# Attention's constants and its first batch prepared inside the expert phase of a two-layer kernel

## The reference, cut to what matters

```python
# layer 0: experts (8 routed, 2 shared), then a ternary projection, added to x
gp = _leaky(jnp.einsum('th,ehm->etm', x, w_gate))
up = jnp.einsum('th,ehm->etm', x, w_up)
y_all = jnp.einsum('etm,emh->eth', gp * up, w_down)
...
x = x + _L0_ffn_ref(_L0_cond_ref(...), packed_weight, weight_scale, bias)

# layer 1: attention, 16 heads of 64, one shared key and value head, one "null" key and value
xn = layernorm(x, g_in)
q = (xn @ Wq).reshape(b, n, H, DH).transpose(0, 2, 1, 3) * scale
kv = xn @ Wkv
k = jnp.concatenate([nk, k], axis=1)      # nk, nv: the null key and value
sim = jnp.einsum('bhid,bjd->bhij', q, k) + bias     # causal and padding masks follow
attn = jax.nn.softmax(sim, axis=-1)
out = jnp.einsum('bhij,bjd->bhid', attn, v)
return layernorm(out.reshape(b, n, INNER) @ Wo, g_out)
...
x = x + _L1_ffn_ref(...)                  # a quantised feed-forward layer
```

## Time and profile before

| | us |
|---|---|
| median of 3 runs (lowest, highest) | 1431.74 (1431.39, 1432.29) |
| the profiled execution | 1432.46 |
| its span in the trace | 1430.5 |

### The profile page before, as it was taken

How to read it: one execution, slowest core, us unless ns; L and a number is a source line. 1 busy time by engine, 2 the same in 40 slices (tenths; PEclk the granted TensorE clock), 3 DMA queues, 4 the chain that set the end, 5 groups by cost and what they waited for, 6 DMA issues and landing times. The chain is left out here.

```text
span 1430.5 us, 29675 instructions
## 1 busy us (share of the span) xinstructions
PE 1251.0 (87%) x8705; PEld 996.3 (70%) x8710; DVE 1029.2 (72%) x2788; ACT 771.5 (54%) x1948; POOL 553.6 (39%) x834
## 2 busy tenths in 40 slices
PE   3999999999945799999999999999999999944866
PEld 2778888888832578777887887778788788831223
DVE  5566666666553877887887778877878878763986
ACT  3223323333312576766776767667667677625853
POOL 1333332333331775444453454444444444500014
PEclk9999999999975899999999999999999999976986
DMA  6233221221025100000000010010010000202115
GB/s 230 70 127 104 83 76 48 103 88 61 28 81 194 53 5 2 1 28 5 2 30 4 2 31 2 1 33 2 1 31 1 17 2 2 76 16 63 59 59 176
DMA packets 51039, 71.52 MB, mean 50 GB/s; under 512 B 4497, under 2 KB 43665, under 8 KB 48850
## 3 DMA queue, kind: packets, MB, share of 16 engines
q1 hardware_dynamic: 50338, 69.60, 14.7%
q10 hardware_dynamic: 560, 0.20, 0.1%
HBM read 57.07 MB, written 12.72 MB: 49 GB/s over the span
## 5 line engine op out<-in xcount | busy, mean ns | idle before, releaser
L864 POOL TENSOR_SCALAR scores<-scores,att_rinv 128x128 f32<-128x128 f32 (+3 forms) x512 | 264.2, 532 | 195.7 <-DVE att_rinv L1076 195.7
L920 ACT ACTIVATE scores<-scores,att_top 128x128 f32<-128x128 f32 (+3 forms) x512 | 281.5, 553 | 77.4 <-DVE att_top L1058 77.1
L1058 DVE CUSTOM_DVE_ANT_0 scores<-ps_y,w_bias_b,null_s 128x128 f32<-128x128 f32 x448 | 229.7, 548 | 83.3 <-PE ps_y L1208 76.8
L271 POOL TENSOR_TENSOR act_w<-act_g,wide_w 128x512 f32<-128x512 f32 x64 | 105.7, 1652 | 261.2 <-DVE act_g L393 255.6
L1207 PE MATMUL ps_y<-k_hh,q_hl 128*128 128x256 f32 (+2 forms) x512 | 190.1, 380 | 14.7 <-DVE att_top L1058 7.3
L928 ACT ACTIVATE keep<-ps_up 128x128 f32<-128x128 f32 (+3 forms) x256 | 112.1, 438 | 167.8 <-PE ps_up L1219 163.9
L1219 PE MATMUL ps_up<-ident,scores 128*128 128x128 f32 x1280 | 190.8, 274 | 9.8 <-DVE keep L1086 9.1
L215 ACT ACTIVATE hid_hi<-hid 128x512 fp32r<-128x512 f32 x80 | 50.6, 632 | 233.9 <-DVE hid L411 229.6
L1219 PEld LDWEIGHTS ps_up<-ident,scores 128*128 128x128 f32 x1280 | 151.3, 141 | 30.9 <-issue 13.7
L1230 PE MATMUL ps_a<-keep,w_val 128*64 128x128 f32 x2560 | 170.7, 280 | 0.7 <-DVE keep L1086 0.7
L871 POOL TENSOR_SCALAR w_q_hm<-q_hl 64x512 fp32r<-64x512 f32 x128 | 76.7, 611 | 228.5 <-ACT q_hl L943 228.5
(11 more groups left out here) (237 smaller groups left out, 2581.6 us busy)
## 6 DMA issues: line engine op xcount, KB each, us to landing
wide_w<-token_w_dram SPq DMA_DIRECT2D x16, 1024.0 KB, 4.7
x_raw<-in_x_t_dram SPq DMA_DIRECT2D x8, 512.0 KB, 3.8
x_nat<-in_x_nat_dram SPq DMA_DIRECT2D x8, 512.0 KB, 4.8
x_dram<-x_nat SPq DMA_DIRECT2D x8, 512.0 KB, 2.9
w_x1t<-x_dram SPq DMA_DIRECT2D x8, 512.0 KB, 4.3
c_dram<-out_raw SPq DMA_DIRECT2D x8, 512.0 KB, 3.2
c2t<-c_dram SPq DMA_DIRECT2D x8, 512.0 KB, 3.7
x_tile<-x_dram SPq DMA_DIRECT2D x8, 512.0 KB, 4.5
```

Source lines behind the costliest of these rows:

```text
L271: nc.gpsimd.tensor_tensor(act_w[:, k % 2], act_g[:, k % 2], wide_w[:, k], ALU.mult).then_inc(sem.act_w_ready, 1)
L864: nc.gpsimd.tensor_scalar(s, s, rinv[:, pp, q, hh:hh + 1], 0.0, ALU.mult, ALU.add).then_inc(sem.p_normed, 1)
L920: nc.scalar.activation(s, s, ACT.Exp, scale=-1.0, bias=top[:, pp, q, hh:hh + 1], accum_out=lsum[:, pp, q, hh:hh + 1]).then_inc(sem.exp_don ...
L1058: dve.tensor_tensor_reduce(scores_of(pp, hh, q), psS[:, hh, 0:n], bias_of(w, h)[:, CAUSAL[q]:CAUSAL[q] + n], 1.0, null_s[:, par, q, h:h + ...
```

## The change

There is no `setup_attention` any more. Its work and attention's serial piece are put into `moe_phase`:

- **The experts' first batch** (`not behind`) gets the constants. DVE signals `raw_free` when the raw expert weights have been split. SP issues `load_projections` behind batch 0's `load_nat`, before `spread_weights(1)`. POOL fills after expert 2 and makes `null_prod` in halves after experts 4 and 6; DVE: `null_picks` behind expert 2, `projections_lo` behind 5, `null_query` behind 6 and 7, `null_rest` behind 9; ACT: `projections_hi` at 4, `null_query_hi` at 7, `null_projected` at 9, each ahead of `hid_hi`; PE: `null_projection` behind `down(7)`.
- **The experts' last batch** (`not ahead`) gets attention's batch 0. SP loads `x1t` before that batch. DVE: norm stages 0 to 2 behind expert 0, 3 to 5 behind 3, 6 and 7 behind 4; then the turns, keys and values in experts 5 to 9 on PE, with ACT's and DVE's splits in the experts after them.
- **The tail** gets the null scores, the turn of them and the first queries ahead of the quantisation.
- **`attention_phase`** starts with its step 0. SP loads the bias of head 2, then batch 1's `x1t`, the mask, and the bias of heads 3 to 15. POOL first fills the second buffers.
- Buffers made early lie over the raw weights (`raw_sb`), and for that the pairs `x_hi`, `x_lo`, `xn_hi`, `xn_lo`, `q_hl`, `q_hm`, `k_hh`, `k_lm` become two tensors each. `y_sb` has a place of its own. The program is built with `dynamic_dma_scratch_size=2048`.

```diff
@@ SP, experts
                     load_nat(b, par)
+                    if isinstance(b, int) and b == 0:
+                        sp.wait_ge(sem.raw_free, 1)
+                        load_projections(sp, dram, w, sem)
...
-                load_projections(sp, dram, w, sem)
                 load_bias(sp, dram, w, range(EARLY), sem)
@@ ACT, experts, inside batch(), ahead of hidden_hi
                         leak_part(s, k % 2)
+                        if not behind and k == 4:
+                            projections_hi()
+                        if not behind and k == 7:
+                            null_query_hi()
+                        if not behind and k == 9:
+                            null_projected()
+                        if not ahead and k == 6:
+                            first.normed_hi(0)
+                        if not ahead and k == 7:
+                            first.normed_hi(1)
+                        if not ahead and k == 8:
+                            first.keys_values()
+                        if not ahead and k == 9:
+                            first.values()
@@ DVE, experts, inside batch()
                         if not (first and k == 0):
                             hidden_lo(s - 1, 1 - k % 2)
+                        if not ahead and k == 6:
+                            ahead_of.normed_lo(0)
+                        if not ahead and k == 7:
+                            ahead_of.normed_lo(1)
+                        if not ahead and k == 8:
+                            ahead_of.keys_lo()
...
                         hidden(b, k)
+                        if first and k == 2:
+                            null_picks()
...
+                        if not ahead and k == 0:
+                            first_norm((0, 1, 2))
@@ DVE, tail
                 hidden_lo(NE * B - 1, 1)
+                ahead_of.query_lo()
                 quantise_scales(B - 1, 1)
@@ PE, experts
+                        if not ahead and k == 5:
+                            first.normed_turn(0)
+                        if not ahead and k == 6:
+                            pe.wait_ge(sem.xnl_ready, 1)
+                            first.normed_turn(1)
+                        if not ahead and k == 7:
+                            first.keys_values()
...
                 batch(B - 1, 1, True, False)
+                first.null_turn()
+                pe.wait_ge(sem.null_s_ready, 1)
+                first.queries()
                 quantised_to_features(B - 1)
@@ SP, attention
+                load_bias(sp, dram, w, range(EARLY, EARLY + 1), sem)
                 load(1)
-                load_bias(sp, dram, w, range(EARLY + 2, NH), sem)
+                sp.dma_start(w.mask[D:D + 1], dram.mask.unsqueeze(0)).then_inc(sem.mask_in, 16)
+                load_bias(sp, dram, w, range(EARLY + 1, NH), sem)
```

More of the change, by code:

```diff
@@ L546, in ternary, with null_projection @@
                     last.then_inc(sem.z_done, 1)
+                def null_projection():
+                    pe.wait_ge(sem.null_pick_ready, 1)
+                    pe.wait_ge(sem.wo_in, 16)
+                    for j in range(PAIRS):
+                        last = pe.matmul(ps.a1[0:NH, 0:H], w.null_pick[:, j * NH:(j + 1) * NH], w.wo[:, j],
+                                         start=(j == 0), stop=(j == PAIRS - 1))
+                    last.then_inc(sem.null_wo_done, 1)
                 def batch(b, par, behind, ahead):
@@ L566, in batch @@
                             ternary(b - 1, 1)
+                        if not behind and k == 7:
+                            null_projection()
+                        if not ahead and k == 5:
[5 more added lines that the diff above has]
+                            first.keys_values()
+                        if not ahead and k == 8:
+                            first.values_turn()
+                        if not ahead and k == NE - 1:
+                            pe.wait_ge(sem.val_ready, 1)
+                            first.null_scores()
                 pe.wait_ge(sem.cond_in, 2 * 16)
```

454 lines of the change are left out of this document (294 added, 160 removed).

## The result

The changed kernel takes 1424.1 us (median of 6 executions, 1423.7 to 1426.9); the kernel before, run beside it, 1431.6 (6 executions, 1430.0 to 1432.8). The ratio is 0.9959, 95% interval [0.9948, 0.9970]: 5.9 us faster (4.3 to 7.4), 7.5 by the difference of the medians. The forecast was 1422.8 in a range of 1412 to 1431. The profiled execution took 1426.2, 2.1 above its own median, with a span of 1424.3: 6.2 less than before.

A forecast was written before the change was run, and what follows sets the result against it. PE was taken as full nearly everywhere except 393 to 465 us, where engines wait in turn; the elementwise ring paces the experts. -42.3 + 4.65 + 2.55 + 12.7 + 2.0 + 7.5 + 4.0 = -8.9: 1431.7 to 1422.8 us, range 1412 to 1431.

The forecast's parts named there:

- Removed, 42.3: Between the experts' end and attention's first step: the setup block and serial piece go, 42.3 us saved.
- The first batch, +7.05: Experts' first batch: making attention's constants there delays the elementwise ring by 7.05 us; POOL's fills and products cost 0.
- The gain at `bias_a`, -2.4: Experts' second batch: bias_a lands before POOL asks for it, since projections are issued earlier; 2.4 us saved.
- The norm, +2.55: Experts' last batch: norm pieces behind experts 0, 3 and 4 exceed DVE's gap of 1.2, costing 2.55 us.
- Experts 6 to 9, +12.7, and the clock, +2.0: Experts' last batch: waits across engines cost 12.7 us, PE's lower clock after idling in expert 8 another 2.0.
- The tail, +7.5: After the last down: query_lo and the steps it needs, ahead of DVE's quantisation, cost 7.5 us (5.3 to 8.4).
- Attention's start, +4.0: Attention's first steps: DVE stalls 4.7 us for batch 1's x1t, 0.7 given back; 4.0 us net, ends 2 and 6.
- Neutral: One barrier less (0.1), y_sb and split tensors without added instructions, smaller DMA scratch priced at 0.
- A (the experts swallow the waits): Rival in the experts: only the moved pieces' true PE work counts, 4.4 us, giving 1410 to 1414; chance 0.12.
- B (little or no difference): Rival for the whole kernel: all cost terms at their upper ends at once, about -1, 1430.5 us; chance 0.11.
- C (the low clock costs 7 in attention): Rival: PE stays at its low level from expert 7 through attention's first steps, +3.3 us or 1435; chance 0.07.
- D: Rival: a buffer laid over raw weights forces a missed wait; 2 in 100, counted in B (little or no difference).

The follow-up runs named there:

- e1: The changed kernel with POOL's null_prod cut to the first of 16 heads, the other 15 left out of the null query: 1420.3 us, ratio 0.9923 to the kernel before.
- e6: The changed kernel with ACT's and DVE's attention pieces in the experts' last batch behind the same expert's hid_hi and hid: 1416.4 us, ratio 0.9901 to the kernel before.
- e8: The changed kernel with 16 more PE matmuls, their result unused, behind the keys and values in the last batch: 1423.3 us, ratio 0.9942 to the kernel before.
- e4: The changed kernel with DVE's query_lo behind the quantisation in the tail instead of ahead of it: 1417.2 us, ratio 0.9904 to the kernel before.
- e5: The changed kernel with batch 1's x1t loaded in the experts' last batch instead of after the barrier: 1420.9 us, ratio 0.9928 to the kernel before.
- e10: The changed kernel with DVE's hid_lo(k - 1) behind hid(k) in batches 0 to 6: 1446.5 us, ratio 1.0108 to the kernel before.
- e7: The changed kernel with projection, picks, query_lo, x1t and ring order moved, null products on DVE, null_query_hi behind hid_hi(9): 1401.6 us, ratio 0.9795 to the kernel before.
- e11: e7 with DVE's hid_lo(k - 1) behind hid(k) in all batches: 1436.2 us, ratio 1.0032 to the kernel before.
- e12: e7 with DVE's hid_lo(k - 1) behind hid(k) only in experts 5 and 6 of batches 0 to 6: 1416.2 us, ratio 0.9902 to the kernel before.

## Why the prediction was right, point by point

The sign and nearly all of the mechanism were right, and the sum is 1.4 us off by the medians, 3.0 by the ratio. Part of that is luck: two terms were too low, by 2.9 and 0.6 us, and two stretches priced at nothing gave back 0.8 and 1.8.

- *Removed, 42.3*: 42.2. Right.
- *The first batch, +7.05*: +9.8 as a rule, +12.1 in the profiled execution. The four waits were about right: the small loads 1.6 (2.0 was taken; its range of 0.5 to 2.6 holds all runs), `projections_lo` 1.3 (1.4), `null_query_hi` 1.75 (1.7), the projection 2.4 (1.8). The step that failed is the sentence on POOL's fills and product halves: "lie in POOL's gap ... 0, at worst 0.5". They lie in POOL's gap, but DVE works in it. They cost 1.5 at expert 5 and 1.75 at expert 7, 3.3 in all (e1). The trace of the kernel before had shown such a hold, in the setup block, DVE and POOL:

```profile
420.13 6.26 DVE L740 TENSOR_SCALAR null_pick<-null_pick,w_null_v 64x8 f32<-64x8 f32 x2
419.88 4.62 POOL L718 TENSOR_TENSOR null_prod<-keep,w_null_k 128x2048 f32<-128x2048 f32 x1 [22.83 <-POOLq L111]
424.56 1.80 POOL L729 MEMSET w_q_hm<- 64x2048 f32 x1
```

  Two operations of eight columns take 6.26 us, where both together take 0.47 in the changed kernel, with no POOL work beside them. The first takes 4.40 and ends with the product, the second 1.85 and ends with the fill behind it. I had read that row only for the time at which PE could start. Against the miss, the routing step of expert 3 was 0.4 shorter than before, since DVE came later to it.
- *The gain at `bias_a`, -2.4*: -2.4. Right.
- *The norm, +2.55*: +2.7. Right.
- *Experts 6 to 9, +12.7, and the clock, +2.0*: 2.6, 2.8, 6.7 and 3.3, together 15.3 against 14.7. The waits are right one by one, with the clock's part in the last two. e6 shows that 7.5 of the 15.3 come from the order of ACT and DVE; the chains through PE, which the text had as the cause of all, are left with 7.8 at most. The clock's 2.0 was low: the two `down` took 1.3 and 1.2 more and the turn of the values 0.69 instead of the 0.35 priced, 2.9 together, though e8 couldn't take them away.
- *The tail, +7.5*: +7.4. Right, and e4 removes all of it. That it is right to 0.1 is chance: over the executions the same code gives 5.6 to 8.1, nearly the ends that the prediction had set (5.3 and 8.4).
- *Attention's start, +4.0*: +4.1. Right in size and cause. Its sentence that with `x1t` in time the sum "would be 4 us better" is a little high: e5 gives 3.0 by step 4 and 3.2 by the median, since a longer hold by POOL takes the stall's place in part.
- *Neutral*: the stretch from batch 1 to 7 became 0.8 us shorter, and what follows attention's step 8 1.8. Neither was in the sum. The first lies in the step from expert 4 to 5 of batches 1 to 6, which is 6.27 us and was 6.39 to 6.66: there DVE no longer idles 0.2 to 0.5 ahead of the routing's sum (L347, now L410); other steps give back 0.5. The second is no larger than what varies: behind step 8 it is 938.7 to 941.7 us in the changed kernel, e1 to e6 and e8 to e10, and 943.5 to 944.3 in the kernel before, e7, e11 and e12. No run isolates either, and their causes stay open. They and the missed 3.3 cancel in part, so the sum is better than its terms.
- *The rivals.* A (the experts swallow the waits) is refuted by the steps of experts 6 to 9. B (little or no difference) didn't occur: 5.9 us is clear of the 2.9 that it allowed. C (the low clock costs 7 in attention) was near its condition, PE not back at the upper level after some 25 us: in the changed kernel the level was 0.50 to 0.57 from 460 to 472 and 1.00 only from 476, 22 us behind the first score. Its price didn't come, the stretch cost 4.1. D didn't occur.

## What to carry to other kernels

A gap of one engine is not free time: ask which other engine works in it and whether both read SBUF, and give the work to the engine whose gap it fills alone; here 2.4 us on POOL became 1.2 on DVE, at no cost where DVE's gap was free. A piece that waits for another engine goes behind the ring's own operation, not ahead of it, and a tail's next-stage work behind the last consumer of this stage; these two orders were worth 7.5 and 7.8 us. Before an operation is moved back, look at what stands behind its consumer in that consumer's fixed order: a saving of 0.4 us per expert cost 14.6.
